# Two attention layers and a mixture of experts on one core: rows of the first eight routed pairs loaded inside attention, a new order of the pairs, and two additions moved to GpSimd

## The chip, the core and the metric

The kernel runs on one core of a Trainium2 chip. The metric is the device time of one execution in microseconds. A core has five engines that run side by side and wait for each other by semaphores: TensorE (PE, with its weight load PEld), VectorE (DVE), ScalarE (ACT), GpSimd (POOL) and SyncE (SP), which issues DMAs.

## The reference, cut to what matters

```python
x = hidden                                   # (4, 1024, 128)
a = x + global_latent_attn(rmsnorm(x, norm1_w), ...)
a = a + local_gqa_attn(rmsnorm(a, norm2_w), ...)
x = layernorm(x + a)
# mixture of experts on the 4096 tokens xt = x.reshape(-1, 128)
shared = silu(xt @ sg_w.T) * (xt @ su_w.T) @ sd_w.T
probs = sigmoid(xt @ router_w.T + routing_bias)          # 8 experts
topk_p, topk_idx = top_k(probs, 2); topk_p /= sum(topk_p)
y_e = silu(xt @ wg[e].T) * (xt @ wu[e].T) @ wd[e].T      # 256 hidden values
x = layernorm(x + shared + sum over the two chosen e of topk_p * y_e)
```

All is float32 in and out. Each token goes through the shared expert and through two of eight routed experts.

## The kernel before, in words

The 4096 tokens are 32 tiles of 128, eight chunks of four tiles. One program has two phases. `attention_layers` runs both attention layers on a clock of steps that is worked out ahead; beside them it already normalises the first six chunks and chooses their experts (parts 0 and 1 of three). GpSimd copies each token's row (the 128 values and four marks) by an indirect DMA to its two places in the DRAM tensor `x_rows`, sorted by expert (`send`, L809, 32 sends of part 0, the last issued at 508.7 us, and the first seven of part 1). Three chunks (`FILLED`, L137: 0, 1, 3) also get their shared expert in there. A barrier ends the phase at about 590 us.

`expert_phase` (L1358) then runs over steps, one pair of 128-token tiles in each. A routed pair takes two blocks of rows from `x_rows`, each with the weights of its expert, whose place comes from a register. A shared pair takes two tiles of tokens in their own order. There are 36 routed pairs and ten shared ones, in the order `SEQUENCE` (L1332): shared 8, routed 0 to 19, shared 9, routed 20 to 35, then shared 10, 11, 4, 5, 12 to 15. In step n the engines do:

- TensorE (L1802): gate and up of pair n (L1750 routed, L1754 shared), transposes of the rows of pair n + 1 (L1771), transposes of the hidden values of pair n - 1 (L1763, routed only), the down product of pair n - 2 (L1796). Tokens of a chunk are transposed once (`turn_tokens`, L1774) at the step in `TURN_AT`; chunk 4's, for shared pairs 8 and 9, ahead of step 0.
- ScalarE: `silu`, the copies of transposed rows and hidden values, and, at the end, normalising a chunk and issuing its store (`normed`, `store_result`).
- VectorE (L1682): multiply of pair n, `read_marks` for a group of four routed pairs (two steps behind the group's first), `move_y` of pair n - 2, then the stages of choosing experts that the tables list, `combine` of a chunk (two additions of the chosen experts' results, at the step in `GATHERED_AT`), its statistics (`end_pair`) and variance (`END_AT`) and, some steps later, its shift.
- SP (L1476): loads the rows of pair m into a ring of eight buffers, for pairs 0 to 35, the first sixteen DMAs right after the phase begins; then, when the sends of a part have landed, the chosen results (`load_chosen`).
- GpSimd: the nine sends of part 1 that are left, the power for the last two chunks' statistics, then per routed pair two indirect DMAs that scatter its results to `y_rows` (`send_y`, L1515). Ahead of pair `FINAL_SENDS` (9) it sends part 2's sixteen row copies (`dispatch`). Powers of the filled chunks stand ahead of pairs 28, 30 and 31, the others behind the last pair.

The last two chunks (6 and 7) leave attention last. The expert phase adds their residual, takes their statistics, lets GpSimd raise them to the power, VectorE make the shift and ScalarE the tokens (`late_tokens`, L1584), and only then chooses their experts. Their shared pairs come last in the sequence. Their chosen results are added before the shared ones (`IN_TIME`), so `move_y` waits for `combine`:

```python
                c = m * 2 // CT
                if c in IN_TIME:
                    dve.wait_ge(f_dve[c], nth(END, "second"))
```

Waits that the steps below name: `turn_rows` waits for the rows of its pair, `load_chosen(part)` for all sends of pairs up to 24, 28 or 36, `combine` for the load of its chunk, `normed` for the shift, `power` for the variance.

## Time and profile before

| | |
|---|---|
| median of 3 runs | 767.56 us (764.21 to 768.39) |
| the profiled execution, its own time | 768.18 us |
| its span, first to last instruction | 766.4 us |
| mean granted TensorE clock over the span | 0.925 |
| busy in the span: PE, DVE, ACT, POOL | 611.2, 509.5, 431.5, 377.0 us |
| expert phase | about 590 to 766 us |

The profile is one execution. Times in its rows are microseconds from the start of the span. A granted clock of 1.00 is the 2.4 GHz level, 0.50 the 1.2 GHz level. In a row of the timeline stand the start, the length, the engine and line, the operation, output and inputs, and in brackets how long the engine was idle before it and what ended that. L160 is a helper through which VectorE's steps go, so its rows are told apart by their tiles.

### The profile page before, as it was taken

Reading aid. Unit: us, or ns where it says so; the run is one execution under the profiler, and the core shown is the slowest. Engines: PE = TensorE matmul, PEld = TensorE weight load, DVE = VectorE, ACT = ScalarE, POOL = GpSimd, SP = SyncE. Lnnn points to the kernel's source line nnn. Section 1 sums busy time; section 2 is a strip of 40 time slices with the busy share of each in tenths; the row PEclk is TensorE's granted clock in tenths of the full one; section 3 lists DMA queues with packets and bytes.
Section 4 is the critical chain, followed back from the end, with each engine's and each line's share of the span. In section 5 each row is a group of like instructions: output and inputs, shape, how many; then the busy total and the mean of one; then the engine's idle time right before and its main releaser. Section 6 shows DMA issues by size and latency. Waiting matters only on the chain. (4 is left out here: it accounts for less than half of the span.)

```text
span 766.4 us, 12178 instructions
## 1 busy us (share of the span) xinstructions
PE 611.2 (80%) x3926; PEld 334.5 (44%) x3926; DVE 509.5 (66%) x1331; ACT 431.5 (56%) x589; POOL 377.0 (49%) x419
## 2 busy tenths in 40 slices
PE   2378888887896987889978586878867899999991
PEld 1213332233443333344424242534656576767681
DVE  2567774476886458799558978447865587633984
ACT  4357776875676765567656355474352553334454
POOL 5365543553535335443143477640356546777751
PEclk9969998998999998899989778899989999999996
DMA  8134565200000000000000001000001422244442
GB/s 260 69 114 170 199 199 190 79 0 1 1 2 1 1 1 15 1 15 15 15 0 1 15 22 43 26 26 1 1 3 52 104 75 77 73 116 140 140 132 69
DMA packets 38125, 47.23 MB, mean 62 GB/s; under 512 B 8960, under 2 KB 35232, under 8 KB 37408
## 3 DMA queue, kind: packets, MB, share of 16 engines
q1 hardware_dynamic: 26976, 35.11, 15.1%
q0 software_dynamic: 4352, 9.05, 3.5%
q10 hardware_dynamic: 6736, 2.30, 1.2%
q8 instruction: 33, 0.54, 0.3%
q14 instruction: 28, 0.23, 0.1%
HBM read 35.30 MB, written 28.98 MB: 84 GB/s over the span
## 5 line engine op out<-in xcount | busy, mean ns | idle before, releaser
L892 ACT ACTIVATE prob<-ps_s 128x1024 f32<-128x1024 f32 x320 | 309.7, 1024 | 163.3 <-PE ps_s L1244 110.7
L1281 PE MATMUL ps_v<-prob,va 128*32 128x512 f32 x1152 | 168.0, 667 | 5.2 <-POOL prob L782 4.5
L1244 PE MATMUL ps_s<-qs,ks 32*128 32x512 f16 x576 | 91.4, 405 | 48.3 <-ACT prob L892 44.9
L782 POOL TENSOR_SCALAR_AFFINE_SELECT prob<-prob 128x1024 f32<-128x1024 f32 x64 | 70.3, 1118 | 54.1 <-ACT prob L892 53.9
L1047 DVE STREAM_TRANSPOSE sums<-ps_v 128x512 f32<-128x512 f32 x62 | 44.2, 713 | 78.9 <-PE ps_v L1281 41.1
L1521 POOL DMA_INDIRECT y_rows<-y,to_row x72 | 70.2, 975 | 38.3 <-DVE y L1643 16.6
L1244 PEld LDWEIGHTS ps_s<-qs,ks 32*128 32x128 f16 x576 | 22.0, 91 | 141.5 <-ACT prob L892 111.1
L1275 PE MATMUL ps_v<-prob,vd 128*128 128x256 f32 (+1 forms) x292 | 64.8, 373 | 14.4 <-DVE marked L1067 14.1
L1554 ACT ACTIVATE gated<-ps_gu 128x512 f32<-128x512 f32 x46 | 27.5, 597 | 78.8 <-PE ps_gu L1750 66.0
L1750 PE MATMUL ps_gu<-weights,rows_t 128*128 x144 | 68.4, 597 | 2.4 <-ACT rows_t L1559 1.9
L1275 PEld LDWEIGHTS ps_v<-prob,vd 128*128 128x128 f32 x292 | 53.4, 207 | 32.1 <-DVE prob L1074 18.4
L699 POOL TENSOR_TENSOR roped<-roped,tsin 128x640 f32<-128x640 f32 x16 | 25.7, 1607 | 61.3 <-DVE tsin L977 50.8
L817 POOL DMA_INDIRECT x_rows<-marked,index x39 | 43.5, 1114 | 16.7 <-issue 15.8
L712 POOL COPY pairs<-pairs 128x128 f16<-128x128 f16 x32 | 10.2, 348 | 80.1 <-DVE pairs L1026 73.8
L1796 PE MATMUL ps_y<-weights,hidden_t 128*128 (+1 forms) x336 | 44.6, 276 | 1.4 <-ACT hidden_t L1568 0.8
L1281 PEld LDWEIGHTS ps_v<-prob,va 128*32 128x32 f32 x1152 | 25.5, 114 | 45.9 <-issue 34.7
L1074 DVE TENSOR_TENSOR prob<-prob,band 128x1024 f32<-128x1024 f32 x32 | 39.2, 1228 | 9.1 <-ACT prob L892 9.1
L1636 DVE TENSOR_TENSOR hidden<-ps_gu,gated 128x512 f32<-128x512 f32 x36 | 24.8, 688 | 30.7 <-PE ps_h L1763 21.8
L1166 PE MATMUL ps_p<-wall,xt 128*128 128x192 f32 x128 | 33.4, 395 | 11.0 <-DVE xt L957 9.5
L1796 PEld LDWEIGHTS ps_y<-weights,hidden_t 128*128 128x128 f32 x336 | 41.0, 192 | 2.4 <-issue 1.8
L1288 PE MATMUL ps_v<-wo,ot 128*128 128x128 f32 x124 | 30.2, 326 | 7.5 <-DVE ot L1061 7.3
L1056 DVE TENSOR_TENSOR on<-sums,rden 128x128 f32<-128x128 f32 x64 | 32.6, 509 | 2.2
(228 smaller groups left out, 1045.3 us busy)
## 6 DMA issues: line engine op xcount, KB each, us to landing
x_rows<-in_blank SPq DMA_DIRECT2D x8, 2112.0 KB, 9.1
rows<-x_rows SPq DMA_DIRECT2D x72, 66.0 KB, 2.1
chosen_y<-y_rows SPq DMA_DIRECT2D x8, 512.0 KB, 4.9
weights<-in_weights SPq DMA_DIRECT2D x1, 3456.0 KB, 13.6
out<-result ACTq DMA_DIRECT2D x8, 256.0 KB, 2.3
marked<-in_hidden SPq DMA_DIRECT2D x3, 512.0 KB, 5.6
r_in<-in_hidden SPq DMA_DIRECT2D x6, 256.0 KB, 2.9
y_rows<-y,to_row POOLq DMA_INDIRECT x72
```

The source lines that it names most:

```text
L782: pool.affine_select(out=probs_at(n, 0, SLOT_COLS), in_=probs_at(n, 0, SLOT_COLS), compare_op=ALU.is_ge, fill=0.0, base=0, pattern=[[0, SL ...
L817: pool.indirect_dma_start(st["x_rows"], bass.IndirectOffsetOnAxis(ap=st["index"][:, t, n:n + 1], axis=0), st["marked"][:, t, :], None).the ...
L892: act.activation(probs_at(n, 0, SLOT_COLS), scores_at(n, 0, SLOT_COLS), ACT.Exp, scale=HD ** -0.5 / GAIN ** 2).then_inc(exped, 1)
L1047: dve.transpose(sums[:].rearrange("p r b v -> p (r b v)"), sums_bank(q).rearrange("p r q -> p (r q)")).then_inc(sums_turned, 1)
L1074: dve.tensor_tensor(probs_at(n, 0, SLOT_COLS), probs_at(n, 0, SLOT_COLS), band[:], ALU.mult).then_inc(banded, 1)
L1166: last = pe.matmul(side_projected(chunk, h)[:, t, 0:PROJ], xt[:, at_col:at_col + P], st["wall"][chunk[0]][:], start=True, stop=True)
L1244: last = pe.matmul(scores_at(n, j * BANK, BANK).rearrange("p (r q) -> p r q", r=REP), ks[b % QUERY_BATCHES][rows, kt * P:(kt + 1) * P], qs ...
L1275: last = pe.matmul(bank[:, :, at_query:at_query + width], vd[b % 2][:, kb, :], probs_at(n, at_col, REP * width).rearrange("p (r q) -> p r ...
L1281: last = pe.matmul(bank[g * VW:(g + 1) * VW, :, :], va[b % VALUE_BATCHES][:, kt, g, :], probs_at(n + g // 2, g % 2 * BANK, BANK).rearrange ...
L1521: pool.indirect_dma_start(y_rows, bass.IndirectOffsetOnAxis(ap=to_row[:, m, t:t + 1], axis=0), y[m][:, t, :], None).then_inc(y_sent[lane], 16)
L1750: last = pe.matmul(ps_gu[n % 2][:, t, :], rows_t[m % 2][:, t, :], weights[:, bass.ds(e, 2 * FF)], start=True, stop=True)
L1796: last = pe.matmul(y_to[:, t, :], hidden_t[n % 2][:, f, t, :], of, start=f == 0, stop=f == 1)
```

## The change

It moves the loads of the first sixteen row blocks (routed pairs 0 to 7) from SP's stream in the expert phase to SP's stream at the end of attention. They wait there for the table of rows of part 0, for part 0's sends and for the last scores of batch 1, since the ring of rows now lies over the queries and keys of batch 1, in one buffer that stays allocated. The sequence becomes routed 0 to 19, shared 8 and 9, routed 20 to 35 and the rest as before; chunk 4's tokens are transposed at step 17. Chunk 0's results are combined at step 32 instead of 31. The dispatch stands ahead of pair 10. For chunks 6 and 7 `combine` leaves VectorE; GpSimd does its two additions, chunk 6's ahead of chunk 2's power and chunk 7's ahead of chunk 6's power. The rest is names (`f_dve` becomes `f_end`).

```diff
@@ attention, SP, behind the wait for the cleared rows
+            row_at = [sp.alloc_register(f"first_row{k}") for k in range(2 * GROUP)]
+            for m in range(RING):
+                if m % GROUP == 0:
+                    sp.wait_ge(p_dve[0], picked(0, "row"))
+                    sp.load(row_at, st["row_table"][0:1, 2 * m:2 * (m + GROUP)])
+                    first_rows = [sp.snap(r, min_val=0, max_val=(X_BLOCKS - 1) * P) for r in row_at]
+                if m == 0:
+                    sp.wait_ge(st["dispatched"][0], 16 * 2 * SHARE_TILES[0])
+                    sp.wait_ge(scored, batch_scored(1))
+                for t in range(2):
+                    sp.dma_start(st["rows"][:, m, t, :], st["x_rows"][bass.ds(first_rows[2 * (m % GROUP) + t], P), :]
+                                 ).then_inc(st["rows_loaded"][m], 16)
@@ tables
-SHARED_FIRST, SHARED_BETWEEN, SHARED_LAST = [8], [9], [10, 11, 4, 5, 12, 13, 14, 15]
-SEQUENCE = ([("shared", j) for j in SHARED_FIRST] + [("routed", m) for m in range(SHARE_PAIRS[FINAL - 1])]
+SHARED_BETWEEN, SHARED_LAST = [8, 9], [10, 11, 4, 5, 12, 13, 14, 15]
+SEQUENCE = ([("routed", m) for m in range(SHARE_PAIRS[FINAL - 1])]
-TURN_AT = {c: SHARED_AT[c * CT // 2] - 3 if c * CT // 2 in SHARED_LAST else -1
-           for c in range(LATE) if c not in FILLED} | {c: LATE_AT + c - LATE for c in range(LATE, CHUNKS)}
+TURN_AT = {c: SHARED_AT[c * CT // 2] - 3 for c in range(LATE) if c not in FILLED} | {c: LATE_AT + c - LATE for c in range(LATE, CHUNKS)}
-GATHERED_AT = {0: 31, 1: 33, 3: 34, 2: 36, 4: 37, 5: 39, 6: 43, 7: 45}
+GATHERED_AT = {0: 32, 1: 33, 3: 34, 2: 36, 4: 37, 5: 39, 6: 43, 7: 45}
+ADDED_BY_POOL = (6, 7)
-POWER_BEFORE = {END_AT[f] - len(SHARED_FIRST + SHARED_BETWEEN) - LAST: f for f in FILLED}
-FINAL_SENDS = 9
+POWER_BEFORE = {END_AT[f] - len(SHARED_BETWEEN) - LAST: f for f in FILLED}
+FINAL_SENDS = 10
@@ expert phase, SP
-            for m in range(PAIRS):
+            for m in range(RING, PAIRS):
@@ expert phase, GpSimd
+            def add_chosen(f):
+                step = Steps(pool, END, f_end[f], lambda n: n)
+                pool.wait_ge(chosen[f], 16)
+                step("first", pool.tensor_tensor, acc[:, chunk(f), :], x[:, chunk(f), :], chosen_y[f][:, :, 0, :], ALU.add)
+                step("second", pool.tensor_tensor, acc[:, chunk(f), :], acc[:, chunk(f), :], chosen_y[f][:, :, 1, :], ALU.add)
...
             for f in results:
                 if f not in FILLED:
+                    for c in [c for c in ADDED_BY_POOL if results.index(f) == results.index(c) - 1]:
+                        add_chosen(c)
                     power(f)
@@ expert phase, ScalarE; TensorE has turn_rows(0) in the same place
-            for c in turned_at(-1):
-                move_tokens(c)
+            move_rows(0)
@@ expert phase, VectorE
-                for f in [f for f, when in GATHERED_AT.items() if when == n]:
+                for f in [f for f, when in GATHERED_AT.items() if when == n and f not in ADDED_BY_POOL]:
                     combine(f, n)
@@ program: one buffer for the queries and keys of batch 1 and the ring of rows
+            second_qk=sb("second_qk", [P, (REP + 1) * S], F16),
+            rows_loaded=[ctx.enter_context(nc.semaphore(f"rows_loaded{p}")) for p in range(RING)],
...
+        qk = st["second_qk"][:]
+        st["rows"] = qk[:, 0:2 * RING * 2 * ROW].bitcast(F32).rearrange("p (m t d) -> p m t d", m=RING, t=2)
```

## Rows read from the trace of the kernel before

**Rows 1.** Busy time by stretch: us, then PE, PEld, DVE, ACT, POOL; PEclk, DMA share, GB/s

```profile
592.00:598.00 6.00, 4.30 (x14) 2.87 (x12) 0.78 (x2) 2.86 (x4) 4.47 (x6) 0.72 0.81 210
...
640.00:700.00 60.00, 60.00 (x331) 41.77 (x330) 31.52 (x87) 24.10 (x53) 44.59 (x47) 1.00 0.35 95
...
710.00:726.00 16.00, 14.71 (x85) 10.23 (x83) 14.72 (x48) 6.63 (x15) 12.12 (x12) 1.00 0.41 141
```

**Rows 2.** Timeline, start of the expert phase: start us, us, engine, line; idle before

```profile
591.73 0.65 PE L1778 MATMUL ps_x<-ident,marked 128*128 128x128 f32 x4 [1.90 <-issue]
...
593.07 3.48 PE L1754 MATMUL ps_gu<-tokens_t,weights 128*128 128x256 f32 x8 [0.69 <-ACT tokens_t L1563]
...
597.05 0.44 PE L1771 MATMUL ps_x<-ident,rows 128*128 128x128 f32 x2 [0.50 <-DMA rows<-x_rows]
...
598.05 1.98 PE L1750 MATMUL ps_gu<-weights,rows_t 128*128 x4 [0.56 <-ACT rows_t L1559]
```

**Rows 3.** Timeline, the first late tokens and the matmuls behind them

```profile
606.06 1.65 ACT L1589 ACTIVATE marked<-marked,l_shift,l_rstd 128x128 f32<-128x128 f32 x4 [1.62 <-DVE l_shift L160]
...
609.73 1.98 PE L1750 MATMUL ps_gu<-weights,rows_t 128*128 x4 [0.50 <-issue]
```

**Rows 4.** Chain that ended last, in order of time: TensorE's pieces of one step

```profile
615.41 0.22 PE ps_x L1771 x2
615.63 0.44 PE ps_h L1763 x4
```

**Rows 5.** Timeline of POOL: first of the last dispatch, first and last send behind it

```profile
643.36 1.07 POOL L1511 DMA_INDIRECT x_rows<-marked,index  x1 [0.30 <-issue]
...
664.49 0.96 POOL L1521 DMA_INDIRECT y_rows<-y,to_row  x1 [0.30 <-issue]
...
738.36 0.95 POOL L1521 DMA_INDIRECT y_rows<-y,to_row  x1 [0.30 <-issue]
```

**Rows 6.** Timeline, the results of the filled chunks

```profile
703.43 13.47 SPq L1474 DMA_DIRECT2D chosen_y<-y_rows  x6
...
706.18 0.60 ACT L1554 ACTIVATE gated<-ps_gu 128x512 f32<-128x512 f32 x1 [1.91 <-PE ps_gu L1750]
...
707.50 0.69 DVE L160 TENSOR_TENSOR acc<-marked,chosen_y 128x512 f32<-128x512 f32 x1 [2.61 <-DMA chosen_y<-y_rows]
...
725.07 1.15 PE L1796 MATMUL ps_y<-weights,hidden_t 128*128 x8 [0.52 <-DVE y L1643]
```

**Rows 7.** Timeline, the tail

```profile
740.67 0.95 SPq L1474 DMA_DIRECT2D chosen_y<-y_rows  x2
...
745.36 0.69 DVE L160 TENSOR_TENSOR acc<-marked,chosen_y 128x512 f32<-128x512 f32 x1
...
746.94 1.01 POOL L1527 TENSOR_TENSOR rstd<-rstd,half 128x4 f32<-128x4 f32 x1 [5.28 <-DVE rstd L160]
...
749.12 0.60 ACT L1554 ACTIVATE gated<-ps_gu 128x512 f32<-128x512 f32 x1 [0.51 <-ACT result L1581]
...
753.26 0.42 DVE L1651 TENSOR_TENSOR acc<-acc,ps_y 128x256 f32<-128x256 f32 x1
...
756.32 0.17 DVE L160 TENSOR_SCALAR rstd<-moments 128x4 f32<-128x4 f32 x1
```

**Rows 8.** One line's instructions: duration in ns min/median/max (GpSimd twice, then VectorE)

```profile
L828 POOL TENSOR_TENSOR kd<-vd x6: 1256/1261/1272, 545.0 to 570.8; 128x512 f32<-128x512 f32 x6
...
L685 POOL TENSOR_TENSOR sq<-marked x16: 1032/1039/2087, 6.8 to 535.8; 128x512 f32<-128x512 f32 x16
...
L1056 DVE TENSOR_TENSOR on<-sums,rden x64: 291/292/2607, 47.3 to 588.7; 128x128 f32<-128x128 f32 x64
```

**Rows 9.** Page, DMA issues: count, KB each, median us from issue to landing

```profile
chosen_y<-y_rows SPq DMA_DIRECT2D x8, 512.0 KB, 4.9
```

**Rows 10.** Timeline, GpSimd's adds beside VectorE at the end of attention

```profile
584.04 2.86 POOL L836 TENSOR_TENSOR marked<-marked,prob 128x256 f32<-128x256 f32 x4
584.04 0.91 DVE L1056 TENSOR_TENSOR on<-sums,rden 128x128 f32<-128x128 f32 x1
```

More of the change, by code:

```diff
@@ L1361, in expert_phase @@
     index, table, x_rows, dispatched = (st[k] for k in ("index", "table", "x_rows", "dispatched"))
+    rows, rows_loaded = st["rows"], st["rows_loaded"]
     late = slice(LATE * CT, CHUNKS * CT)
@@ L1383, in expert_phase @@
         acc = sb("acc", [P, TILES, D])
-        rows = sb("rows", [P, RING, 2, ROW])
         rows_t = [sb(f"rows_t{p}", [P, 2, P]) for p in range(2)]
@@ L1408, in expert_phase @@
         p_dve, p_exped, p_ranked = (st[n] for n in ("p_dve", "p_exped", "p_ranked"))
-        rows_loaded = [sem(f"rows_loaded{p}") for p in range(RING)]
         marks_read = sem("marks_read")
@@ L1417, in expert_phase @@
         chosen = [sem(f"chosen{f}") for f in range(CHUNKS)]
-        f_dve = [sem(f"f_dve{f}") for f in range(CHUNKS)]
+        f_end = [sem(f"f_end{f}") for f in range(CHUNKS)]
         f_rstd, f_result, out_stored = sem("f_rstd"), sem("f_result"), [sem(f"out_stored{p}") for p in range(RESULTS)]
@@ L1484, in _ @@
                         sp.wait_ge(flown[lane], 16 * len(range(lane, 2 * SHARE_TILES[FINAL], FLYING)))
-                elif m == 0 or m in SHARE_PAIRS:
+                elif m in SHARE_PAIRS:
                     sp.wait_ge(dispatched[part_of(m)], 16 * 2 * SHARE_TILES[part_of(m)])
@@ L1523, in send_y @@
                     ).then_inc(y_sent[lane], 16)
+            def add_chosen(f):
[3 more added lines that the diff above has]
+                step("second", pool.tensor_tensor, acc[:, chunk(f), :], acc[:, chunk(f), :], chosen_y[f][:, :, 1, :], ALU.add)
             def power(f):
-                pool.wait_ge(f_dve[f], nth(END, "var_eps"))
+                pool.wait_ge(f_end[f], nth(END, "var_eps"))
                 pool.tensor_tensor(rstd[f][:], rstd[f][:], st["half"][:, 0:CT], ALU.pow).then_inc(f_rstd, 1)
@@ L1577, in normed @@
                 place = results.index(f)
-                act.wait_ge(f_dve[f], nth(END, "shift"))
+                act.wait_ge(f_end[f], nth(END, "shift"))
                 after(act, out_stored[place % RESULTS], 16 * (place // RESULTS))
@@ L1617, in end_step @@
             def end_step(f):
-                return Steps(dve, END, f_dve[f], lambda n: n)
+                return Steps(dve, END, f_end[f], lambda n: n)
             def end_pair(f, pair):
@@ L1647, in move_y @@
                 if c in IN_TIME:
-                    dve.wait_ge(f_dve[c], nth(END, "second"))
+                    dve.wait_ge(f_end[c], nth(END, "second"))
                 base = acc if c in IN_TIME else x
@@ L1799, in _ @@
             load_weights(0)
-            for c in turned_at(-1):
-                turn_tokens(c)
+            turn_rows(0)
             for n in STEPS:
@@ L1929, in program @@
                   multiples=views["multiples"].rearrange("p (e m) -> p e m", e=EXPERTS))
+        qk = st["second_qk"][:]
+        st["rows"] = qk[:, 0:2 * RING * 2 * ROW].bitcast(F32).rearrange("p (m t d) -> p m t d", m=RING, t=2)
         with ExitStack() as both:
             st.update(
-                qs=[both.enter_context(nc.sbuf_tensor(f"qs{b}", [P, REP, S], F16)) for b in range(QUERY_BATCHES)],
-                ks=[both.enter_context(nc.sbuf_tensor(f"ks{b}", [P, S], F16)) for b in range(QUERY_BATCHES)],
+                qs=[qk[:, 0:REP * S].rearrange("p (r s) -> p r s", r=REP) if b == 1 else
+                    both.enter_context(nc.sbuf_tensor(f"qs{b}", [P, REP, S], F16))[:] for b in range(QUERY_BATCHES)],
+                ks=[qk[:, REP * S:] if b == 1 else both.enter_context(nc.sbuf_tensor(f"ks{b}", [P, S], F16))[:]
+                    for b in range(QUERY_BATCHES)],
                 kd=[both.enter_context(nc.sbuf_tensor(f"kd{p}", [P, BLOCKS_OF_KEYS, P], F16)) for p in range(2)],
```

## The prediction

> **What bounds the kernel now.** I first read the busy time by stretch, cut at the change's three places. From 592 to 598 us (start of the expert phase) TensorE is busy 4.30 of 6 us at a mean granted clock of 0.72; from 640 to 700 it is busy 60.00 of 60 us, so what others do there can cost but not gain; from 710 to 726 it lacks 1.29 us and VectorE is the busiest [rows 1]. The rows before 590 us belong to attention, which the change touches only through SP and the address of one buffer. Then the timeline of each place and the waits in it.
>
> **Part 1: rows loaded inside attention, routed pairs first.** Removed is the wait of the first routed pair's transposes for its rows: 0.50 us, and 0.56 us behind it for the copy on ScalarE [rows 2]. That is not 4 us, though the rows took about that long: the shared pair ran meanwhile, its eight matmuls in 3.48 us at the low clock, and the new first pair has the same columns to multiply at the same clock. The sixteen loads go to a time when SP and the DMA engines are idle; SP has them issued long before attention ends, so they cost nothing; if they came late, the first pair would wait as now.
>
> What the new order gives at the start: two transposes instead of four (0.65 us for four [rows 2]) and a copy half as wide put the first matmul some 0.35 us earlier. But TensorE soon stands behind another chain. Statistics of the last two chunks go VectorE, GpSimd, VectorE, ScalarE; ScalarE's four token instructions start at 606.06 and the matmuls behind them at 609.73 [rows 3]. This chain hangs on VectorE's first multiply, 0.35 us earlier, and gets the first reading of the marks in front of it (four small instructions, partly in VectorE's idle time): I take 0.2 us earlier. At that point the new order has one routed pair more behind it and one shared pair more still to do. A routed pair has two row transposes and four of the hidden values more than a shared one, 0.22 and 0.44 us [rows 4]; but four transposes of chunk 4, now at step 17, cost twice 0.22 at full clock. Net 0.22. **Start: 0.4 us**, between nothing and 1.1 (the whole of both waits).
>
> **Part 2: sends and the dispatch.** The dispatch before pair 10 instead of 9 stands at the same step as before, since the pairs come one step earlier; it starts 0.4 us earlier. GpSimd has no slack behind it: from 664.49 to 738.36 it sends 27 pairs, 54 sends, nearly back to back, the dispatch's sixteen before them also (643.36 to 664.49, 1.3 us each) [rows 5]. Now 26 pairs are left: two sends fewer, each 0.96 us and 0.30 of idle time behind it, 2.5 together. So every later send comes 2.5 + 0.4 = 2.9 us earlier, and with it what SP loads behind the sends.
>
> **Part 3: results of chunk 0 at step 32.** Now SP issues the first result's load at 703.43, it is there at 707.50 and VectorE has waited 2.61 us; from then on it works without a gap until its product lets TensorE go on at 725.07, which is late by 0.52 us [rows 6]. After: the load at 700.5, there at 704.6. The same instructions follow in another order, and now begin with step 32's multiply, behind the gate's 0.60 us at 706.18 [rows 6], less 0.4 for the start: 706.4. That is 1.1 us before 707.50, so TensorE goes on at 724.0. **Up to here: 1.05 us**, the start's 0.4 in it. Bounds of the middle's share: nothing (steps 32 to 34 now hold three combines and two statistics close together), and 1.29 us, all of TensorE's gaps [rows 1].
>
> **Part 4: GpSimd adds the results of chunks 6 and 7.** VectorE loses four additions of 0.69 us. The first two run from 745.36 and stand ahead of a shift, so of ScalarE's normalising, so of the last gate at 749.12 and the last multiply behind it; the other two stand directly ahead of 753.26. VectorE's last variance, at 756.32, has then only GpSimd's power, the shift, four activations and the store behind it [rows 7]. If GpSimd is in time and in nobody's way, the last gate comes by the first two additions earlier, 1.35 us, and the rest by the other two, 1.3: 2.65 us, with the 1.05 above **3.7 us**.
>
> Is GpSimd in time? An addition of two different inputs of this size took it 1.26 us; one with a single input read twice took 1.04, once 2.09 [rows 8]. I take 1.26, the same form, and keep 1.04 and 2.09. SP issues the last two loads at 740.67 [rows 7], now 737.8; with 4.9 us to land [rows 9] the first is there at 742.7 and added at 745.25; the power of chunk 2 (1.01 us [rows 7]) follows, then chunk 7, done by 748.9. VectorE asks for them at about 746 and 750. Both in time, with 0.8 and 1.1 us to spare.
>
> Is it in nobody's way? VectorE's multiply of two SBUF inputs usually takes 0.29 us, and took up to 2.61 [rows 8]; beside GpSimd's adds one took 0.91 [rows 10]. In the tail VectorE's shifts read two SBUF inputs too (its other large instructions there read PSUM or a single input). Chunk 4's shift would be due at 744.4 and waits for the running add until 745.25: 0.85 us, which goes through ScalarE's normalising to the last gate. Chunk 5's shift meets chunk 7's adds: nothing if it gets in between the two, 0.65 if not; I take half. **Sum: 3.7 - 0.85 - 0.3 = 2.5 us.** The profiled execution took 768.18 us, so 765.7; the median of the runs is 0.62 us lower, which gives **765.1 us**.
>
> By the Trainium skill (SBUF — State Buffer, the section on SBUF's two separate sides) VectorE and GpSimd share a port pair under an exclusive lock: an instruction of VectorE with two SBUF inputs and one of GpSimd that reads SBUF don't overlap, the later waits for the whole of the other. By this rule the time is the 765.1 just given, without it the 763.9 below; the 0.91 us agrees with it, which is why I hold the blocked case the likelier.
>
> **Rivals.**
> A, the forecast: 765.1, by itself between 764.2 and 766.5 (either shift blocked or not, start between 0 and 0.8). Chance 0.40.
> B, the adds block nothing, because they fall between the shifts: 3.7 us, 763.9. For it: the shifts are few and small (128x4, as the variance of 0.17 us [rows 7]), and a load that lands 1 us later moves the adds off them. If the start also gives its upper bound, it is 763.2. Chance 0.30.
> C, slower: GpSimd is late. VectorE must wait for its second add before it may add the last matmuls' results. If the loads don't come earlier (there at 745.6) and an add takes 2.09, chunk 6 is done at 749.8, the power at 750.9, chunk 7 at 755.1; VectorE's two last pairs take from there the 3.06 us of 753.26 to 756.32 [rows 7] and end at 758.2, 1.9 us later than now: 769.5. It decides from the point where chunk 7's second add ends behind 753.3. Against it: GpSimd has nothing else to do at that time: ahead of its power at 746.94 it is idle for 5.28 us [rows 7]. Chance 0.14.
> D, the early parts give nothing: the second pair, too, runs at the low clock (1.5 us more, 3.48 against 1.98 [rows 2]) or VectorE's denser steps 32 to 35 take back what the start gave. Then only the tail's 1.5 us or less are left: 766.1 to 767.6. Chance 0.16.
>
> **The numbers.** A measurement of this kernel can tell about 0.5%, 3.8 us, from no change: faster is below 763.7, slower above 771.4. Faster: 0.22 of B's 0.30 (any 0.2 us more from the start suffices) and 0.08 of A, where small terms err together: 0.30. Slower: 0.06, the end of C in which also the middle stalls. Same: 0.64. The range leaves out 0.08 below and 0.12 above: 762.9 (B with its bounds) to 768.6.
>
> **What would show it.** The first routed matmul near 592.7 in place of 598.05, at the low clock; no wait for rows; the matmuls behind the first late tokens at about 609.5. The last send near 735.4 and the last result loads near 737.8. No idle time of VectorE ahead of the first chosen addition; TensorE going on at 724.0. GpSimd's four adds of 1.26 us ending near 745.3 and 748.9; a shift of over 0.5 us beside them (A) or none (B); the last variance near 753.8. A wait of VectorE for GpSimd ahead of the last matmul results means C. What would prove the whole wrong is a gain or loss inside attention, whose end I expect unmoved at 590 us.

## The result, and the profile after

| | before | after |
|---|---|---|
| median of 20 runs, us | 766.13 (762.95 to 769.5) | 762.67 (758.91 to 765.96) |
| ratio, 95% interval | | 0.9952 [0.9938, 0.9967] |
| span of the profiled execution, us | 766.4 | 760.9 |
| a second set: 27 and 12 runs, us | 766.19 | 761.18, ratio 0.9946 [0.9925, 0.9968] |

The change makes the kernel 3.5 us faster, 0.5%. The forecast was 765.1 with a range from 762.9: the gain was larger than the 2.5 us forecast, and 762.67 lies just below the range. The three runs that the forecast counted from had a median 1.43 us above that of the twenty; counted from the twenty, the range would begin at 761.5 and hold the result.

**A clock for the comparison.** The two spans differ by 5.5 us, more than the change gives. SP's issue of `x_in` is the first instruction behind the barrier, and the last issue of a store ends the work. The timeline has them, first two rows before, last two after:

```profile
590.53 0.37 SPq L1466 DMA_DIRECT2D x_in<-in_hidden  x1
...
759.48 0.38 ACTq L1573 DMA_DIRECT2D out<-result  x1
```

```profile
588.29 0.40 SPq L1477 DMA_DIRECT2D x_in<-in_hidden  x1
...
754.01 0.38 ACTq L1592 DMA_DIRECT2D out<-result  x1
```

From one to the other it is 168.95 us before and 165.72 after: 3.23 us are the expert phase's. The other 2.24 lie ahead of the barrier, in attention. The change touches attention by SP's sixteen loads, which stand at 509 us in the timeline after, and by the address of one buffer:

```profile
509.46 9.39 SPq L677 DMA_DIRECT2D second_qk<-x_rows  x16
```

If VectorE's instructions of the two traces are matched in their order, those after come 2.2 us earlier from 100 us of the span on, and still 2.2 us at 575. So the loads did not make them. Further profiles of kernels with the same loads and the same buffer differ as much from one another: kernels with the changed attention have the `x_in` issue at 585.42, 585.55, 590.26 and 590.87, kernels with the old one at 590.98 and 590.75. All times called "phase" below count from that issue.

**The start of the phase after**, timeline of PE and ACT, against [rows 2, 3]:

```profile
590.43 3.65 PE L1768 MATMUL ps_gu<-weights,rows_t 128*128 x4 [0.56 <-ACT rows_t L1578]
593.92 0.38 PE L1789 MATMUL ps_x<-ident,second_qk 128*128 128x128 f32 x2
595.13 1.98 PE L1768 MATMUL ps_gu<-weights,rows_t 128*128 x4 [0.82 <-ACT rows_t L1578]
...
603.60 1.65 ACT L1608 ACTIVATE marked<-marked,l_shift,l_rstd 128x128 f32<-128x128 f32 x4 [2.08 <-DVE l_shift L160]
...
606.60 1.88 PE L1768 MATMUL ps_gu<-weights,rows_t 128*128 x4
```

The first gate-up is a routed pair and starts at phase 2.14 instead of 2.54. No wait for rows is left. The late tokens come at phase 15.31 (15.53 before), but the gate-up matmuls behind them at 18.31 instead of 19.20: before, TensorE had 0.50 us by "issue" (a wait for nothing that the profile shows) in front of them [rows 3], which is gone.

**Stretches after**, same columns as [rows 1], cut 2 us earlier:

```profile
590.00:596.00 6.00, 4.74 (x8) 2.04 (x9) 1.25 (x2) 2.45 (x4) 4.55 (x5) 0.72 0.43 131
638.00:698.00 60.00, 60.00 (x339) 42.96 (x338) 30.68 (x83) 24.83 (x54) 45.66 (x48) 1.00 0.33 91
708.00:724.00 16.00, 14.90 (x83) 10.15 (x82) 14.76 (x47) 6.34 (x13) 11.78 (x12) 1.00 0.31 99
```

TensorE is full in the middle as before. Between 708 and 724 it still lacks 1.10 us of 16. The timeline of that place, VectorE's stretch with its first chosen addition and TensorE's gaps, against [rows 6]:

```profile
703.91 0.69 DVE L1654 TENSOR_TENSOR hidden<-ps_gu,gated 128x512 f32<-128x512 f32 x1 [1.92 <-PE ps_h L1781]
...
705.74 0.68 DVE L160 TENSOR_TENSOR acc<-marked,chosen_y 128x512 f32<-128x512 f32 x1
...
708.10 0.42 DVE L1661 TENSOR_TENSOR y<-ps_y,of_weight 128x256 f32<-128x256 f32 x1 [0.23 <-PE ps_y L1814]
...
717.28 0.66 PE L1781 MATMUL ps_h<-ident,hidden 128*128 128x128 f32 x4 [0.31 <-DVE hidden L1654]
...
721.91 1.15 PE L1814 MATMUL ps_y<-weights,hidden_t 128*128 x8 [0.79 <-ACT hidden_t L1587]
...
731.12 1.13 PE L1814 MATMUL ps_y<-weights,hidden_t 128*128 128x128 f32 x8 [0.22 <-DVE y L1661]
```

Before, TensorE had one gap more than [rows 6] show:

```profile
711.00 1.15 PE L1796 MATMUL ps_y<-weights,hidden_t 128*128 x8 [0.77 <-ACT hidden_t L1568]
```

VectorE no longer waits for the load. TensorE's gaps are 0.31, 0.79 and 0.22 where they were 0.77 and 0.52. VectorE's packed stretch begins with step 32's multiply at phase 115.62, 1.35 us earlier than with the first addition before (116.97), but it now waits 0.23 us for TensorE on its way and still holds TensorE up.

**The tail after**, timeline, against [rows 5, 7]:

```profile
733.44 0.95 POOL L1532 DMA_INDIRECT y_rows<-y,to_row  x1 [0.30 <-issue]
...
735.83 0.91 SPq L1485 DMA_DIRECT2D chosen_y<-y_rows  x2
...
739.84 1.27 POOL L160 TENSOR_TENSOR acc<-marked,chosen_y 128x512 f32<-128x512 f32 x1 [0.94 <-DMA chosen_y<-y_rows]
741.19 1.27 POOL L160 TENSOR_TENSOR acc<-acc,chosen_y 128x512 f32<-128x512 f32 x1
742.36 0.17 DVE L160 TENSOR_SCALAR rstd<-moments 128x4 f32<-128x4 f32 x1
742.44 0.16 DVE L160 SCALAR_TENSOR_TENSOR shift<-moments,rstd 128x4 f32<-128x4 f32 x1
742.61 1.02 POOL L1544 TENSOR_TENSOR rstd<-rstd,half 128x4 f32<-128x4 f32 x1
742.84 0.69 DVE L1654 TENSOR_TENSOR hidden_t<-ps_gu,gated 128x512 f32<-128x512 f32 x1 [0.24 <-PE ps_y L1814]
743.60 1.28 POOL L160 TENSOR_TENSOR acc<-marked,chosen_y 128x512 f32<-128x512 f32 x1
744.86 0.14 DVE L160 SCALAR_TENSOR_TENSOR shift<-moments,rstd 128x4 f32<-128x4 f32 x1
744.96 1.27 POOL L160 TENSOR_TENSOR acc<-acc,chosen_y 128x512 f32<-128x512 f32 x1
...
744.80 0.60 ACT L1573 ACTIVATE gated<-ps_gu 128x512 f32<-128x512 f32 x1 [0.51 <-PE ps_gu L1772]
...
750.85 0.17 DVE L160 TENSOR_SCALAR rstd<-moments 128x4 f32<-128x4 f32 x1
```

Rows of GpSimd and VectorE are put in order of time here. The variance at 742.36 is chunk 2's, the shifts at 742.44 and 744.86 are chunk 4's and chunk 5's. The last send stands at phase 145.15 (147.83 before), the last loads at 147.54 (150.14). GpSimd's four adds take 1.27 or 1.28 us. **Both shifts are 0.16 and 0.14 us long, and nothing holds them**: chunk 4's begins 0.02 us before the second add ends (741.19 + 1.27 = 742.46), chunk 5's 0.02 before the next ends (744.88). The last variance is at phase 162.56, before at 165.79.

Where the 3.23 us came in, read as the phase time of the same point in both traces: gate of step 3, 0.23; step 5, 0.64; step 33, 0.66; TensorE's last gate-up, 0.81; last gate, 2.08; last variance, 3.23.

### The profile page after: what moved, and what is told of

The parts are those of the page before. It is cut to its first block and busy times, and to the rows that moved or that the text cites. A ratio compares the mean times of both kernels' runs of the same rounds, so it can differ in the third digit from the quotient of the medians.

```text
span 760.9 us, 12178 instructions
## 1 busy us (share of the span) xinstructions
PE 608.4 (80%) x3926; PEld 332.9 (44%) x3926; DVE 506.5 (67%) x1327; ACT 431.8 (57%) x589; POOL 381.6 (50%) x423
## 5 line engine op out<-in xcount | busy, mean ns | idle before, releaser
L1256 PE MATMUL ps_s<-qs,ks 32*128 32x512 f16 x432 | 70.3, 409 | 34.5 <-ACT prob L904 32.0
L1768 PE MATMUL ps_gu<-weights,rows_t 128*128 x144 | 70.2, 611 | 2.2 <-ACT rows_t L1578 2.2
L1256 PEld LDWEIGHTS ps_s<-qs,ks 32*128 32x128 f16 x432 | 16.8, 91 | 106.2 <-ACT prob L904 82.6
L724 POOL COPY pairs<-pairs 128x128 f16<-128x128 f16 x32 | 10.2, 348 | 80.8 <-DVE pairs L1038 74.4
```

The costliest lines, as they stand in the source:

```text
L1256: last = pe.matmul(scores_at(n, j * BANK, BANK).rearrange("p (r q) -> p r q", r=REP), ks[b % QUERY_BATCHES][rows, kt * P:(kt + 1) * P], qs ...
L1768: last = pe.matmul(ps_gu[n % 2][:, t, :], rows_t[m % 2][:, t, :], weights[:, bass.ds(e, 2 * FF)], start=True, stop=True)
```

## The experiments

The runs fell on five chips, of two kinds. On two of them (and where the result above was measured) the kernel before takes 766 us; on the other three some 799. "First chip" and "second chip" in the expectations mean one of the first and one of the second kind. On the second kind all kernels stand still for 20 us and more around steps 13 to 15, which lets GpSimd's sends catch up, and lose some more around steps 38 to 40, so the middle and the arrival of the last loads are other cases there (told at the end). Of the kernels that ran on the first kind, only before and after have two profiles there; the others have one. Durations of instructions and the order in the tail can be read on both; where it mattered a kernel was run again.

### Each half alone

Adds alone: the kernel before with only this.

```diff
+ADDED_BY_POOL = (6, 7)
+            def add_chosen(f): ...
+                    for c in [c for c in ADDED_BY_POOL if results.index(f) == results.index(c) - 1]:
+                        add_chosen(c)
```

> The kernel before, with only the additions of chunks 6 and 7 moved to GpSimd. Measured from SP's load of the last chunks' hidden values to the last store's issue, the expert phase took 168.95 us before and 165.72 after the whole change. Theory: the additions pay only with the sends that the other parts bring forward. Here the last two loads are issued some 150.1 us into the phase as before, GpSimd ends chunk 6's second add near 157.5, and VectorE stands and waits for it ahead of step 44's last matmul results, for 0.5 to 2 us. Phase 167.7 to 168.7, so 0.2 to 1.2 us shorter than before. Rival: the additions give their gain by themselves, no wait of VectorE for GpSimd of over 0.2 us, phase 166.3 to 166.8.

On the second kind: 798.05 us, ratio 0.9981 [0.9953, 1.0009]. The last loads were issued at phase 173.45 there and the adds were in time; the last variances stood 5.24 and 3.25 us apart as in the kernel after. The expected wait needs GpSimd's backlog of sends, which only the first kind has, so it was run again:

> The kernel before with the adds of chunks 6 and 7 on GpSimd and nothing else, a second time, on the same chip. There the last loads of chosen rows are issued 2.5 us later than in the kernel after. Theory: chunk 6's rows land at 155.1 us of the phase, GpSimd's two adds end at 157.8, VectorE waits about 0.5 us for them or not at all, and the phase is 166.5 to 167.6. Rival (the adds need the earlier sends): VectorE waits 1.5 us or more for GpSimd, phase 168 or more.

On the first kind: 765.28 us, ratio 0.9992 [0.9964, 1.0019]; to the last store issue 167.34, last variance 164.17, TensorE's last gate-up at 154.99. Timeline of GpSimd, then of VectorE:

```profile
744.77 1.27 POOL L160 TENSOR_TENSOR acc<-marked,chosen_y 128x512 f32<-128x512 f32 x1 [2.99 <-DMA chosen_y<-y_rows]
746.12 1.27 POOL L160 TENSOR_TENSOR acc<-acc,chosen_y 128x512 f32<-128x512 f32 x1
747.35 1.02 POOL L1534 TENSOR_TENSOR rstd<-rstd,half 128x4 f32<-128x4 f32 x1
748.34 1.27 POOL L160 TENSOR_TENSOR acc<-marked,chosen_y 128x512 f32<-128x512 f32 x1
```

```profile
745.53 0.54 DVE L160 TENSOR_SCALAR rstd<-moments 128x4 f32<-128x4 f32 x1
745.98 0.15 DVE L160 SCALAR_TENSOR_TENSOR shift<-moments,rstd 128x4 f32<-128x4 f32 x1
746.05 0.68 DVE L1645 TENSOR_TENSOR hidden_t<-ps_gu,gated 128x512 f32<-128x512 f32 x1
747.49 0.42 DVE L1660 TENSOR_TENSOR acc<-acc,ps_y 128x256 f32<-128x256 f32 x1 [0.76 <-POOL acc L160]
...
748.92 0.71 DVE L160 SCALAR_TENSOR_TENSOR shift<-moments,rstd 128x4 f32<-128x4 f32 x1
```

Here the adds come later against VectorE's steps. The variance takes 0.54 us instead of 0.17 and ends at 746.07, 0.03 behind GpSimd's first add; VectorE waits 0.76 for the second; chunk 5's shift takes 0.71 instead of 0.14 and ends at 749.63, 0.02 behind the add that ran (748.34 + 1.27). From TensorE's last gate-up to the last variance it is 9.18 us, against 10.70 before and 8.28 after. The theory's 166.5 to 167.6 us holds, with a somewhat longer wait; the rival's does not. The first expectation, 167.7 to 168.7, was too long.

No adds: the kernel after with `ADDED_BY_POOL = ()`.

> The changed kernel, with the additions of chunks 6 and 7 left on VectorE. Theory: the start, the order and the middle bring TensorE's last gate matmuls 0.5 to 0.8 us forward and nothing behind them changes: phase 168.1 to 168.5 against 168.95 before and 165.72 after. Rival: the earlier sends are worth something in the tail without GpSimd's adds: phase below 167.5.

Second kind: 799.22 us, ratio 0.9993 [0.9963, 1.0022]; the last four variances 6.43, 6.38 and 3.24 us apart. Run again:

> The kernel after with the adds of chunks 6 and 7 back on VectorE, a second time, for a chip on which the kernel before takes 766 us. Theory (the four adds of 0.69 us on VectorE are what the tail lost): the phase from SP's issue of x_in to the last store issue is 2.3 to 2.7 us longer than the kernel after's 165.2 to 165.7, that is 167.6 to 168.4, and the last variances stand 6.38 us apart instead of 5.24. Rival (the early parts carry the gain): under 1 us longer.

First kind: 766.78 us, ratio 1.0003 [0.9978, 1.0027]. To the last store issue 168.01, last variance 164.85, with 6.38 us between the variances of chunks 2 and 6 (before 6.37); TensorE's last gate-up at 154.25, so 10.60 from there. The theory holds: without the adds the kernel is 2.29 us behind the kernel after, at the lower edge of the 2.3 to 2.7 forecast. The medians don't resolve a part of a microsecond (0.94 us are inside the interval); the phase clock does.

The kernels before and after, unchanged, again:

> The kernel before, unchanged, for a second profile. Theory (the gate of step 0 and all that hangs on it vary by half a microsecond from one execution to the next, in both kernels): the first gate of the expert phase lies between 5.8 and 6.8 us after SP's issue of x_in, and steps 3 and 5 are 0.1 to 0.7 us away from 17.09 and 24.92. Rival: they repeat within 0.1 us, and the start of the kernel after is really 0.6 to 1.1 us shorter.

Last variance 165.98, last store issue 169.14, gates of steps 3 and 5 at 17.02 and 24.82: they repeat within 0.1 us, as the rival said. TensorE's last gate-up comes 0.29 us later than in the first profile, so differences of the middle below some 0.3 us are not told apart by one profile each.

> The kernel after, unchanged, on the chip of the runs above. Theory (the gain is the early steps' 0.2 to 0.9 us and the 3 us or so of VectorE's final adds): 3 to 4 us below the kernel before, near 794 to 795 where before is 798, with the last three variances 5.24 and 3.25 us apart. Rival (the gain needs the backlog of sends that only the first chip shows): under 1.5 us below.

This one fell on the first kind, not on the one that its numbers were meant for: 761.18 us, ratio 0.9946 [0.9925, 0.9968], 5.0 us below the kernel before by the medians (2.4 to 5.7 by the interval). Step 0 of the phase at 5.34 instead of 5.84, all later points 0.50 earlier, last variance 162.07.

| first kind of chip, phase us | step 3 gate | last gate-up, PE | last gate | last variance | gate-up to variance |
|---|---|---|---|---|---|
| before | 17.09 | 155.09 | 158.59 | 165.79 | 10.70 |
| before again | 17.02 | 155.38 | 158.78 | 165.98 | 10.60 |
| adds alone | 17.04 | 154.99 | 157.58 | 164.17 | 9.18 |
| after, no adds | 16.84 | 154.25 | 157.65 | 164.85 | 10.60 |
| after | 16.86 | 154.28 | 156.51 | 162.56 | 8.28 |
| after again | 16.36 | 153.79 | 156.02 | 162.07 | 8.28 |
| after, adds pushed back | 16.40 | 153.82 | 156.69 | 162.89 | 9.07 |
| after, both early | 16.41 | 153.73 | 155.95 | 162.01 | 8.28 |

### Do GpSimd's adds hold VectorE?

The kernel after with one more add of half the size ahead of each chunk's two, into the same place, so that the following ones start later:

```diff
                 pool.wait_ge(chosen[f], 16)
+                half = slice(f * CT, f * CT + CT // 2)
+                pool.tensor_tensor(acc[:, half, :], x[:, half, :], chosen_y[f][:, 0:CT // 2, 0, :], ALU.add).then_inc(half_added, 1)
+                pool.wait_ge(half_added, 1 + ADDED_BY_POOL.index(f))
```

> The kernel after with one more add of half the size (128x256, the same values to the same place) ahead of the two adds of each of chunks 6 and 7 on GpSimd, about 0.7 us each, so that a shift of VectorE, which in the kernel after begins within 0.02 us of the end of an add, falls into the middle of one. Theory of the prediction (a small two-input operation of VectorE waits while GpSimd adds): that shift starts or ends only with the add, 0.4 to 0.8 us after the statistics before it instead of 0.32, and the final steps behind it are as much later. Rival (nothing is held): the shift stays 0.31 to 0.32 us behind the last statistics and 0.14 to 0.17 us long, and the variances stay 5.24 and 3.25 us apart.

First kind: 761.55 us, ratio 0.995 [0.9924, 0.9977]. Timeline of VectorE's small instructions, then of GpSimd's adds:

```profile
743.87 0.82 DVE L160 TENSOR_SCALAR rstd<-moments 128x4 f32<-128x4 f32 x1
744.61 0.15 DVE L160 SCALAR_TENSOR_TENSOR shift<-moments,rstd 128x4 f32<-128x4 f32 x1
...
746.69 1.17 DVE L160 SCALAR_TENSOR_TENSOR shift<-moments,rstd 128x4 f32<-128x4 f32 x1
```

```profile
743.40 1.27 POOL L160 TENSOR_TENSOR acc<-acc,chosen_y 128x512 f32<-128x512 f32 x1
...
746.58 1.27 POOL L160 TENSOR_TENSOR acc<-marked,chosen_y 128x512 f32<-128x512 f32 x1
```

The prediction's mechanism is real. The variance becomes 0.82 us long and ends at 744.69, 0.02 behind the add (744.67); chunk 5's shift becomes 1.17 us and ends at 747.86, 0.01 behind the other (747.85). The last gate is 0.67 us and the last variance 0.82 later than in the repeat of the kernel after, which started alike (steps 3 to 33 within 0.04). VectorE's multiplies and additions with one input in PSUM and its statistics beside the same adds keep their usual lengths.

By the Trainium skill (SBUF — State Buffer, "Who interferes with whom") VectorE and GpSimd have one port pair under a lock that the first comer keeps for its whole instruction; an instruction with two SBUF inputs, as a shift is, contends for it, and a `tensor_scalar` can in one of its faster modes. The trace agrees, for both forms, with the 0.82, 1.17, 0.54 and 0.71 us above.

### Two causes that I suspected in the traces

Moving chunk 0 from step 31 to 32 also moves its shift, so that ScalarE's normalising stands in front of the silu of step 40, which comes 0.36 us later than before although step 39 came 1.00 earlier. Shift one step earlier:

```diff
-END_STEPS = {f: 6 for f in FILLED} | {4: 6, 5: 4, 2: 3, 6: 2, 7: 1}
+END_STEPS = {f: 6 for f in FILLED} | {0: 5, 4: 6, 5: 4, 2: 3, 6: 2, 7: 1}
```

> The kernel after with the shift of chunk 0, and with it the normalising, one step earlier (END_STEPS for chunk 0: 5 instead of 6). Theory: in the kernel after, ScalarE's two normalising passes of chunk 0 stand before the silu of step 40 and hold its gate back by 1.36 us, of which 0.5 us is left from step 41 on; moved a step earlier they lie where they lay in the kernel before, so the gate of step 40 comes 1 us or more earlier and the phase from SP's issue of x_in to the last store issue shortens from 165.7 to 165.2 us. Rival: the passes delay whatever silu stands behind them alike, and the 0.5 us is lost elsewhere: phase 165.7, with the bump only moved to step 39.

Second kind: 795.45 us, ratio 0.998 [0.9951, 1.0009]; no answer, since the sends had no backlog. In the next kernel it stands together with TensorE's register load of expert numbers one step earlier:

```diff
-                if n + 2 < len(SEQUENCE) and routed(n + 2) and SEQUENCE[n + 2][1] % GROUP == 0:
-                    load_weights(SEQUENCE[n + 2][1])
+                if n + 3 < len(SEQUENCE) and routed(n + 3) and SEQUENCE[n + 3][1] % GROUP == 0:
+                    load_weights(SEQUENCE[n + 3][1])
```

> The kernel after with two edits: the shift of chunk 0 a step earlier and TensorE's register load of expert numbers a step earlier. Theory: the two delays that the kernel after still has are worth 0.5 us (normalising ahead of a silu) and up to 0.4 us (a gap of TensorE by issue ahead of the tokens' turn), so 0.5 to 0.9 us below the kernel after. Rival: both lie beside waits for the late tokens or for chosen rows, and the time is that of the kernel after within 0.3 us.

First kind: 762.66 us, ratio 0.9965 [0.9941, 0.999]. Gate of step 40, first in this kernel, then in the repeat of the kernel after (their `x_in` issues are at 585.55 and 585.42):

```profile
727.75 0.60 ACT L1573 ACTIVATE gated<-ps_gu 128x512 f32<-128x512 f32 x1 [1.94 <-PE ps_gu L1772]
```

```profile
728.86 0.60 ACT L1573 ACTIVATE gated<-ps_gu 128x512 f32<-128x512 f32 x1 [0.53 <-ACT result L1600]
```

The gate does come 1.24 us of the phase earlier, but TensorE's last gate-up only 0.06, and so does the last variance. One TensorE step ahead of that gate is 0.11 us shorter (2.97 against 3.08, as in the kernel before); from there on TensorE runs back to back, 2.62 us a step, and does not wait for that gate. My theory fell: a silu that is late is not a step that is late. The register load gave nothing either; steps 3 to 33 lie within 0.05.

The register load by itself, in the kernel before:

> The kernel before with each register load of expert numbers on TensorE one step earlier (n + 3 instead of n + 2). Theory: of the 0.89 us by which the early part of the kernel after gained behind the late tokens, 0.50 is this load, exposed on TensorE behind the stalled turn of the tokens in the kernel before; moved away from there the gate of step 4 comes 0.4 to 0.5 us earlier against x_in's issue, and the phase goes from 168.95 to 168.5 us. Rival: the load is hidden in the clock's and the tokens' wait and costs nothing: gate of step 4 unchanged, phase 168.9.

> The kernel before with TensorE's register load of expert numbers a step earlier, on a chip where the kernel before takes 766 us. Theory (0.5 us of the kernel after's gain at step 4 is this load, no longer exposed behind the late tokens): the gap of 0.50 us by issue ahead of the gate-up matmuls of step 4 is gone, the gates from step 4 on come 0.4 to 0.5 us earlier against x_in's issue, and the last variance comes at 165.3 to 165.6. Rival: the gap moves to another wait behind the late tokens and the gates from step 5 on stay at 24.8 to 24.9.

Both fell on the second kind: 799.36 us, ratio 1.0011 [0.998, 1.0041], and 800.06, ratio 1.0019 [0.9997, 1.0042]. TensorE's timeline in the second, then in a kernel of the same order with the load in its old place (rows alone, second run, below), which kept the low clock as long:

```profile
604.12 1.98 PE L1750 MATMUL ps_gu<-weights,rows_t 128*128 x4 [0.82 <-issue]
...
611.25 1.88 PE L1750 MATMUL ps_gu<-weights,rows_t 128*128 x4
```

```profile
611.56 1.98 PE L1769 MATMUL ps_gu<-weights,rows_t 128*128 x4 [0.45 <-issue]
```

The gap in front of the gate-up behind the late tokens is gone, and step 4's gate comes 3.37 us behind step 3's, as in the kernels with the new order. With the load in its old place it is 4.10 (mean of three kernels on the first kind) and 4.09 in the kernel with the same low clock, so the clock does not make the difference: the load does. Step 5's gate is 7.37 us behind step 3's against 7.79. The 0.82 us by "issue" ahead of step 2, where the load now stands, are no new cost: the kernel before has 0.82 there too, put down to ScalarE's copy. The theory holds up to step 5; behind it the 20 us stop leaves no answer.

### Rows alone, chunk 0's step, the dispatch

The kernel before with the early row loads and nothing else:

> The kernel before, with only the loads of the first eight pairs' rows moved into attention; order, steps, dispatch and additions as before. Theory: the first routed pair's gate is 0.4 to 0.6 us earlier, and from step 4 on everything stands where it stood, within 0.15 us, because the late tokens' chain sets the time there: phase 168.8 to 169.0. Rival: the 0.50 and 0.56 us that TensorE waited are kept to the end: phase 167.9 to 168.3.

> The kernel before with the rows of the first eight pairs loaded inside attention, the old order, the old steps and the adds on VectorE, on a chip where the kernel before takes 766 us. Theory (the late tokens' chain anchors step 3): step 1 comes 0.4 us earlier, step 3 not at all, and the last variance stays within 0.2 us of before's 165.8 to 166.0. Rival (the removed wait is kept): steps 3 to 33 0.4 us or more earlier and the last variance at 165.4 or less.

Both on the second kind: 797.81 us, ratio 0.9984 [0.9957, 1.0012], and 798.5, ratio 0.9992 [0.9968, 1.0015]. In the first, steps 1 and 3 have their gates at 9.16 and 17.17, and step 4 ran its gate-up at the low clock again (3.27 us); in the second the low clock lasted into step 1 and they are at 11.48 and 18.16. What answers is the adds-alone kernel, which has the old loads but happened not to wait for its rows: on the first kind its steps 1 and 3 are at 9.04 and 17.04, in the two profiles of the kernel before, with a wait of 0.50 and 0.58, at 9.53 and 9.55, and at 17.09 and 17.02. So step 1 comes 0.5 us earlier without the wait and step 3, which hangs on the late tokens, does not: the wait by itself was worth nothing by then.

The kernel after with chunk 0 combined at step 31 again:

```diff
-GATHERED_AT = {0: 32, 1: 33, 3: 34, 2: 36, 4: 37, 5: 39, 6: 43, 7: 45}
+GATHERED_AT = {0: 31, 1: 33, 3: 34, 2: 36, 4: 37, 5: 39, 6: 43, 7: 45}
```

> The changed kernel, with chunk 0's results combined at step 31 as before instead of 32 (its statistics, shift and normalising with it). Theory: moving chunk 0 by a step made VectorE's steps 33 to 36 denser and put its normalising between the gates of steps 39 and 40, where ScalarE held the gate of step 40 back by 1.3 us against the pace (gain 1.00 us at step 39, minus 0.36 at step 40, 0.52 from step 41 on). With the sends 2.9 us earlier the load is there in time for step 31. So 0.5 to 1.3 us come back: phase 164.4 to 165.2. Rival: VectorE waits for the load at step 31 as it did before (over 1 us) and the phase is 165.7 or longer.

> The kernel after with the first results (chunk 0) combined at step 31, as in the kernel before, instead of 32, on a chip where the kernel before takes 766 us. Theory (the middle gave 0.2 us where 0.65 was forecast because that step moved, which put the first add of chosen rows at 117.0 to 117.5 us of the phase, no earlier than before's 117.0): the first add comes 1 us or more earlier, TensorE's three gaps shrink from 1.32 us in all, and the last variance comes 0.3 to 0.6 us earlier than after's 162.1 to 162.6. Rival (VectorE's order with the multiplies decides, not the start): the gaps stay at 1.2 to 1.4 us and the last variance within 0.15 us.

> The kernel after with chunk 0 combined at step 31 instead of 32, a third time, hoped for on a chip where the kernel before takes 766 us. Theory (the moved step held the middle's gain at 0.2 us): the first add of chosen rows before 116 us of the phase, TensorE's gaps between 700 and 732 us under 1.0 us in all, the last variance at 161.5 to 162.0. Rival: gaps of 1.2 to 1.4 us, the last variance at 162.0 to 162.6.

All three on the second kind: 796.97, 793.62 and 794.3 us, ratios 0.9965 [0.9933, 0.9998], 0.9925 [0.9899, 0.995] and 0.9944 [0.9918, 0.9969]. It is faster than the kernel before there too. Whether it beats the kernel after stays open: the two were never timed on the same chip.

The kernel after with `FINAL_SENDS = 9`:

> The kernel after with the dispatch of the last tokens ahead of pair 9 instead of 10, so that it stands in front of one pair more and each send of the final part comes as late as the order of pairs makes it. Theory (the gain of the adds hangs on when they begin): if the last two loads of chosen rows are issued later than 147.5 us of the phase, the adds run into VectorE's small instructions, which are then held 0.4 us or more each, and the last variance comes up to 1 us later than after's; the total number of sends behind the dispatch is 27 pairs again, so 2.5 us later is expected for the loads, 149.6 to 150.1, and 163.3 to 163.9 for the last variance. Rival: the order around the dispatch changes nothing behind it, loads at 147.1 to 147.5 and the last variance at 162.1 to 162.6.

> The kernel after with the last dispatch ahead of pair 9 instead of 10, a second time, hoped for on a chip where the kernel before takes 766 us. Theory: the loads of the last chosen rows are issued at 149.6 to 150.1 us of the phase, the adds on GpSimd hold VectorE's small instructions as in the run with the adds alone, and the last variance is at 163.1 to 163.9. Rival: loads at 147.1 to 147.5 and the last variance at 162.1 to 162.6.

Second kind again: 797.9 us, ratio 0.9988 [0.9957, 1.0018], and 799.75, ratio 0.9989 [0.9958, 1.0019]. The last loads are issued at phase 178.03 and 179.71, behind the 20 us stop, so the question (how much the tail owes to the earlier sends) got no answer this way. The adds-alone kernel answers it: with the sends 2.5 us later the same adds gave 1.4 to 1.5 us instead of 2.3 to 2.4.

## Why the prediction was wrong

The step that failed is the tail's subtraction: 0.85 us for chunk 4's shift held by GpSimd's add and 0.3 for chunk 5's. In the kernel after neither shift was held, 0.16 and 0.14 us long, and the tail gave 2.4 us where 1.5 was left of its 2.65. The other terms were off too, and in part cancelled.

**The start: 0.4 forecast, 0.6 measured.** The late tokens came 0.22 us earlier, as worked out. Behind them came 0.67 more, 0.50 of it TensorE's gap by issue, which the prediction had among its rows [rows 3] and did not price: the register load above. At step 5, 0.64 were left. Of the five profiles with the new order on the first kind, two have 0.64 and 0.67 us there and three 1.09 to 1.14; in the three the first gate-up took 3.2 us, in the two 3.6, all of them partly at the low clock.

**The middle: 0.65 forecast, 0.25 measured.** At TensorE's first gate-up behind the packed stretch the gain is 0.91, from 0.66 at step 33; a step with a gap of 0.22, 0.11 longer than the same step before, leaves 0.81. The wait for the load went as forecast, but VectorE did not run from there without a gap. The loads came 2.6 us earlier, near the 2.9, though by other pieces: the dispatch began 1.1 us earlier in the phase, not 0.4, and GpSimd, which was to have no slack, then waited once for VectorE, 2.38 us. The sum up to here, 0.81 against 1.05 forecast, was near because the start gave more and the middle less; over all profiles of the first kind it is 1.2 (the three with the old order have the last gate-up at 155.15 on average, the five with the new at 153.97).

**The tail: 2.65 less 1.15 forecast, 2.4 measured.** The four additions off VectorE are 2.32 to 2.42 us (10.60 or 10.70 against 8.28), near the 2.65. VectorE now waits for TensorE there (0.24 us at 742.84), and the variances of chunks 2 and 6 stand 5.24 us apart, two of TensorE's steps of 2.62. The prediction took away 0.85 for chunk 4's shift and 0.3 for chunk 5's. The lock behind these terms exists, and its price when it strikes is near: 0.8 us with the adds pushed back, 0.9 with the adds alone, that together with a wait. But it does not strike in the kernel after. The loads landed 4.0 us after their issue (735.83 to 739.84), not 4.9 [rows 9], a figure from all eight; so the adds began 0.6 us sooner than forecast (739.84 + 2.24 is 742.08 on the clock of before, forecast 742.7), the second ended at 744.70, and chunk 4's shift was due at 744.68, not at 744.4. That is luck: a few hundredths of a microsecond, and an arrival that the median of the loads did not give. Chunk 5's shift misses for a firmer reason. GpSimd's power stands behind chunk 2's variance and chunk 7's first add behind the power, so the add ends 2.52 us after that variance begins; the shift begins 2.50 after it (744.88 and 744.86 from 742.36). The ten profiles in which nothing pushes the adds back, both kinds of chips among them, all have the shift 0.01 or 0.02 us ahead of the add's end. With the adds alone on the first kind the power had to wait for chunk 6's second add, and the shift was caught. The rows of before would have said otherwise:

```profile
746.70 0.16 DVE L160 TENSOR_SCALAR rstd<-moments 128x4 f32<-128x4 f32 x1
...
748.86 0.14 DVE L160 SCALAR_TENSOR_TENSOR shift<-moments,rstd 128x4 f32<-128x4 f32 x1
```

There the shift begins 2.16 us after the variance, which puts it 0.36 inside the add. It is the new wait of VectorE for TensorE ahead of the multiply between them that carries it past; the prediction did not look at that wait.

**The rivals.** B, the adds block nothing, came true: 3.7 us forecast, 3.2 to 3.9 measured between issue and store (two profiles of each kernel). Its argument was a load that lands later; it landed sooner. C did not occur in the kernel after; its wait, 0.76 us, appears when the adds are taken without the earlier sends. D's mechanism, the second pair at the low clock too, is real on the second kind (below), with the old order as well (three of five profiles there), and not in any profile of the first kind.

**The base.** Counted from 766.13 the forecast would have been 763.6 and rival B 762.4; measured 762.67. The sign that was to prove the whole wrong, an end of attention away from 590 us, did come (588.29), but the 2.2 us are there 400 us ahead of the changed loads.

So the two halves of the change help each other. Alone, the early rows and the order give 0.9 us and the adds 1.6 (last variance 164.85 and 164.17 against 165.79); together they give 3.2, 0.7 more than the sum, because the sends that come 2.5 us earlier spare VectorE the wait for GpSimd's second add and move the adds out of the way of its small instructions. These are one profile each; with the repeats the whole is 3.2 to 3.9.

## What to carry to other kernels

When work goes to GpSimd beside VectorE, list VectorE's SBUF-only instructions that come due while it runs, the small ones above all: a 0.14 us shift became 1.17. What decides here is a margin of hundredths of a microsecond, so follow both chains back to their last common event, and count the waits that the change itself creates: the distances of the old trace gave the wrong order for chunk 5's shift. If one of the chains hangs on a DMA, keep both cases. Compare traces from the first instruction behind a barrier, not from the start of the span.

## What the runs showed of the hardware

- **The held instruction ends with the add**, 0.01 to 0.03 us behind its end in four of four cases. In the kernel after, a variance that began 0.10 us before an add's recorded end was not lengthened, in two other profiles one that began 0.13 before. Either the add frees the way a little before its record ends, or the variance asks for it a little after its record begins; no run tells these apart.
- **Low clock at the start.** In the kernel after the clock is back at 2.4 GHz 5 to 6 us into the phase. On the second kind five of seven profiles of kernels with the new order, and three of five with the old, kept 1.2 GHz to phase 10 or 11. Mean granted clock is the figure before the last two, the kernel after first, then the one with chunk 0's shift early:

```profile
593.00:595.00 2.00, 1.31 (x4) 0.37 (x2) 0.24 (x1) 0.87 (x2) 1.68 (x2) 0.79 0.21 68
595.00:597.00 2.00, 1.87 (x5) 0.87 (x6) 1.93 (x4) 0.00 (x0) 1.41 (x2) 1.00 0.21 68
```

```profile
595.00:597.00 2.00, 2.00 (x5) 0.72 (x3) 0.00 (x0) 0.12 (x1) 1.39 (x3) 0.50 0.22 68
599.00:601.00 2.00, 2.00 (x4) 0.79 (x3) 1.80 (x6) 0.00 (x0) 1.59 (x2) 0.50 0.21 68
```

- **A stop of 20 us on the second kind of chip.** There TensorE, ScalarE and VectorE stand for long stretches of 642 to 670 us, in every kernel, during the last sixteen dispatch DMAs, while GpSimd goes on. TensorE's timeline in the kernel with chunk 0's shift early and the busy times of the kernel without adds:

```profile
667.94 3.77 PE L1768 MATMUL ps_gu<-weights,rows_t 128*128 x4 [10.40 <-issue]
```

```profile
642.00:670.00 28.00, 13.02 (x57) 8.37 (x55) 8.46 (x32) 3.66 (x8) 20.56 (x22) 0.73 0.21 66
```

The waits are put down to "issue" and not to any engine of the kernel. The DMA view shows the instruction queues' reads of that time at 646 to 652 us in the kernel after, on the first kind, and in the stopped kernel none from 640 to 658. That the engines waited for their code is a guess that fits; no run tested it. VectorE's multiplies of steps 37 and 39, 7.0 or 7.1 us apart on the first kind, are 10.2 to 10.9 apart on the second; the cause of that is open as well.
